# Fewer picked columns at the end of a layer, and their bank emptied earlier, in a three-layer graph attention kernel

## The reference

```python
h = relu(layernorm(x))
for l in range(3):
    f_out = (nf @ W_ni)[src] + (nf @ W_nj)[dst] + ef @ W_fij + bias
    f_out = leaky_relu(f_out, 0.2).reshape(-1, 4, 32)
    e = einsum('ehd,hd->eh', f_out, attn)
    a = exp(e - segment_max(e, dst)[dst]);  a = a / segment_sum(a, dst)[dst]
    m = (nf @ W_node).reshape(-1, 4, 32)[src] * a[:, :, None]
    nf, ef = segment_sum(m, dst).mean(axis=1), f_out.mean(axis=1)
out = x + nf
```

## Time and profile before

| | |
|---|---|
| median of 3 runs | 3021.41 us (3011.55 to 3023.02) |
| the profiled execution's own time | 3008.55 us |
| its span, first to last instruction | 3006.7 us |
| instructions | 50077 |
| TensorE's mean granted clock | 0.843 of 2.4 GHz |
| gathers (L554) | 1995, 1889.3 us busy |
| pick matmuls (L664) | 6345, 630.0 us busy |
| make_hot compares (L1360) | 705, 181.1 us busy |
| pick_rows copies (L1374, L1378) | 141 and 564, 33.0 and 155.3 us busy |

### The profile page before, as it was taken

One profiled execution on the slowest core, in us unless ns is written; L12 is line 12 of the kernel. 1 busy time (PEld: TensorE's weight loads), 2 busy tenths in 40 slices (PEclk: granted clock), 3 DMA queues, 4 the chain that ended last, 5 costly groups with the idle time before them and its releaser, 6 DMA issues.

```text
span 3006.7 us, 50077 instructions
## 1 busy us (share of the span) xinstructions
PE 2404.8 (80%) x15871; PEld 1878.0 (62%) x16027; DVE 2490.5 (83%) x6428; ACT 1447.6 (48%) x3416; POOL 2058.9 (68%) x2167
## 2 busy tenths in 40 slices
PE   3388888888887378888888887649999888998984
PEld 1366667676764356667766665337777777776753
DVE  7399999999997468998999998637888888879784
ACT  0155555555555135555556555414445454445452
POOL 6777777777770577777777776377776666667653
PEclk9699988888899589987999999857778787778796
DMA  6235454535342324343435342332333343333222
GB/s 252 64 96 156 122 147 116 152 110 158 110 128 85 112 74 142 119 149 110 157 111 158 110 153 98 118 103 67 100 120 99 98 136 98 108 108 100 91 92 81
DMA packets 139275, 353.92 MB, mean 118 GB/s; under 512 B 43895, under 2 KB 96027, under 8 KB 120207
## 3 DMA queue, kind: packets, MB, share of 16 engines
q1 hardware_dynamic: 67216, 296.09, 27.9%
q0 software_dynamic: 68960, 39.71, 8.6%
q10 hardware_dynamic: 2838, 14.91, 1.3%
HBM read 137.79 MB, written 212.77 MB: 117 GB/s over the span
## 4 chain that ended last, share of the span: by engine, by line
PE 39%; DVE 29%; issue 14%; ACT 9%; POOL 5%; DMA 3%; SPq 1%; DVEq 0%; ACTq 0%; POOLq 0%
DVE U L1349 12%; PE f_ps L695 12%; PE pick_ps L664 10%; PE f_ps L704 9%; PE xT_ps L685 5%; DVE rows L1266 4%; DVE lr L1277 4%; DVE U L1334 3%; POOL rows L554 2%; ACT f_low L850 2%; ACT xT L841 2%; ACT up L901 2%; PE f_ps L714 2%; ACT wide_ps L889 1%; DVE rows L1378 1%
## 5 line engine op out<-in xcount | busy, mean ns | idle before, releaser
L554 POOL DMA_INDIRECT rows<-nf_tab,src_sb x1995 | 1889.3, 947 | 706.9 <-issue 574.9
L704 PEld LDWEIGHTS f_ps<-w_out,lr 128*128 128x128 f32 x4836 | 701.0, 210 | 379.0 <-issue 277.3
L664 PE MATMUL pick_ps<-nf_part,z 125*128 125x160 bf16 x6345 | 630.0, 264 | 258.4 <-issue 217.0
L1349 DVE TENSOR_TENSOR_SCAN U<-wide_ps,U 128x272 f32<-128x272 f32 (+2 forms) x1272 | 801.6, 694 | 3.2 <-ACT wide_ps L889 2.4
L695 PE MATMUL f_ps<-xT,w_edge 97*128 97x512 f32 x1212 | 753.8, 708 | 22.6 <-ACT ef_new L872 12.0
L664 PEld LDWEIGHTS pick_ps<-nf_part,z 125*128 125x128 bf16 x6345 | 564.6, 112 | 289.8 <-issue 241.3
L704 PE MATMUL f_ps<-w_out,lr 128*128 128x36 f32 (+1 forms) x4836 | 649.8, 274 | 31.2 <-DVE lr L1277 28.8
L1277 DVE TENSOR_TENSOR lr<-f_ps,f_low 128x512 f32<-128x512 f32 x606 | 410.0, 677 | 252.4 <-ACT f_low L850 247.0
L850 ACT ACTIVATE f_low<-f_ps 128x512 f32<-128x512 f32 x606 | 361.0, 596 | 495.9 <-PE f_ps L695 495.9
L685 PE MATMUL xT_ps<-ident,rows 128*97 128x128 f32 x2418 | 431.8, 305 | 76.8 <-issue 37.2
L841 ACT ACTIVATE xT<-xT_ps 97x512 f32<-97x512 f32 x606 | 358.8, 592 | 147.8 <-PE xT_ps L685 145.6
(11 more groups left out here) (163 smaller groups left out, 1070.5 us busy)
## 6 DMA issues: line engine op xcount, KB each, us to landing
u_tab<-up SPq DMA_DIRECT2D x144, 1088.0 KB
s_nd<-edge_first SPq DMA_DIRECT2D x48, 768.0 KB
rows<-nf_tab,src_sb POOLq DMA_INDIRECT x1995, 2.5
ef_tab<-ef_new SPq DMA_DIRECT2D x32, 768.0 KB
ef_st<-ef_tab SPq DMA_DIRECT2D x32, 768.0 KB
z<-fifth_tab SPq DMA_DIRECT2D x141, 96.0 KB
edge_first<-s_nd ACTq DMA_DIRECT2D x16, 768.0 KB
ef_st<-in_edge_attr_dram SPq DMA_DIRECT2D x16, 672.0 KB
```

The source lines that it names most:

```text
L554: eng.indirect_dma_start(rows[q % RING][:, c * K:c * K + D], None, nf_tab[:, :], bass.IndirectOffsetOnAxis(ap=src_sb[:, t:t + 1], axis=0)) ...
L664: mm = eng.matmul(pick_ps[:, i * PB:(i + 1) * PB], hot[m % 2][0:NQ, f * PW + i * P:f * PW + (i + 1) * P], nf_part[a][0:NQ, f * PB:(f + 1) ...
L704: mm = eng.matmul(f_ps[n % 2][:, u * m:(u + 1) * m], lr[y][:, u * P:(u + 1) * P], w_out[l][:, 0:m], start=True, stop=True)
L1349: last = eng.tensor_tensor_scan(uh[:, c0 * w:c1 * w], dbc[h % 2][:, 0:(c1 - c0) * w], uh[:, c0 * w:c1 * w], 0.0, ALU.mult, ALU.add)
```

## The change

`PICK_LESS = [12, 2, 2]`: in layer 0 the last 12 of the 47 sub-blocks with picks have none, in layers 1 and 2 the last two. So `NPICKS` is 35, 45 and 45. GpSimd gathers those columns (48 more in all), and TensorE runs `warm` in those steps. The running number of a picked sub-block, on which buffers and semaphore values rest, comes from `pick_no`. On VectorE `pick_rows` is put right behind `leaky` of step i = 2, ahead of the two `add_up`; it was behind them.

```diff
@@ -31,6 +31,7 @@
 PARTS5 = 5
 SPLITS = 3
 IDXB = 4
+PICK_LESS = [12, 2, 2]
 SLOPE = 0.2
 WARM_UP = 16
 KEEP_WARM = 4
@@ -66,6 +67,7 @@
     HALF = [(0, D // 2), (D // 2, C)]
     END = NG - 18
     NPICK = END // GB + 1
+    NPICKS = [NPICK - PICK_LESS[l] for l in range(L)]
     assert NCOL == PARTS5 * PARTS5
     assert NQ * NCOL == N and HD == P and FULL < P and E < P * T
 
@@ -336,17 +338,20 @@
         def ef_in_count(q):
             return 16 * sum(ef_loads(a) for a in range(q % 2, q + 1, 2))
 
-        def picks(g):
-            return g % GB < PICK and g // GB < NPICK
-
-        def is_picked(t):
-            return t % GT == 2 and picks(t // GT)
-
-        def gathered(g):
-            return grp_w(g) - picks(g)
+        def picks(l, g):
+            return g % GB < PICK and g // GB < NPICKS[l]
+
+        def pick_no(l, b):
+            return sum(NPICKS[:l]) + b
+
+        def is_picked(l, t):
+            return t % GT == 2 and picks(l, t // GT)
+
+        def gathered(l, g):
+            return grp_w(g) - picks(l, g)
 
         def rows_sem_to(q, a):
-            return 16 * sum(gathered((v % NS) * GS + a)
+            return 16 * sum(gathered(v // NS, (v % NS) * GS + a)
                             for v in range(q % RING, q + 1, RING)
                             if (v % NS) * GS + a < NG)
 
@@ -413,7 +418,7 @@
                                   ).then_inc(ef_out[q % 2], 16)
 
                 def load_fifths(l, b):
-                    m = l * NPICK + b
+                    m = pick_no(l, b)
                     if m >= IDXB:
                         eng.wait_ge(hot_made, PARTS5 * (m - IDXB + 1))
                     eng.dma_start(fifths[m % IDXB],
@@ -494,7 +499,7 @@
                             load_ef(q0 + s + 2)
                         for b in range(max(SUBS * s - 2, 0), SUBS * s + 1):
                             store_u(k0 + b)
-                            if b + IDXB + 2 < NPICK:
+                            if b + IDXB + 2 < NPICKS[l]:
                                 load_fifths(l, b + IDXB + 2)
                     for b in range(SUBS * (NS - 1) + 1, NB):
                         store_u(k0 + b)
@@ -540,7 +545,7 @@
                 def gather_cols(l, cols):
 
                     for t in cols:
-                        if is_picked(t):
+                        if is_picked(l, t):
                             continue
                         q, c = l * NS + t // SUP, t % SUP
                         if c == 0 and q >= RING:
@@ -675,8 +680,8 @@
                             eng.wait_ge(dst_spread, (q + 1) * D)
                             eng.wait_ge(ef_put, q + 1)
                         eng.wait_ge(src_rows[q % RING][a], rows_sem_to(q, a))
-                        if picks(g):
-                            eng.wait_ge(picked, PARTS5 * (l * NPICK + g // GB + 1))
+                        if picks(l, g):
+                            eng.wait_ge(picked, PARTS5 * (pick_no(l, g // GB) + 1))
                         if n >= 2:
                             eng.wait_ge(xT_ready, n - 1)
                         else:
@@ -720,7 +725,7 @@
                     for g in range(-2, END - 2):
                         turn(g + 2)
                         b, i = g // GB + 2, g % GB
-                        if g >= 0 and i < PICK and b < NPICK:
+                        if g >= 0 and i < PICK and b < NPICKS[l]:
                             pick(b, i)
                         elif g >= 1:
                             warm(g + 1, FILL_STEADY)
@@ -1390,6 +1395,8 @@
                     for g in range(-1, END - 2):
                         b, i = g // GB - 1, g % GB
                         leaky(g + 1)
+                        if g >= 0 and i == PICK - 1 and b + 3 < NPICKS[l]:
+                            pick_rows(b + 3)
                         if b >= 0:
                             if i == 0:
                                 soften(b)
@@ -1401,9 +1408,7 @@
                             else:
                                 add_up(b, 2)
                                 add_up(b, 3)
-                        if g >= 0 and i == PICK - 1 and b + 3 < NPICK:
-                            pick_rows(b + 3)
-                        if g >= 0 and i == 0 and b + 4 < NPICK:
+                        if g >= 0 and i == 0 and b + 4 < NPICKS[l]:
                             make_hot(b + 4)
                         if 0 <= g and g // GS + 1 < NS:
                             s, a = g // GS + 1, g % GS
```

## The result

The changed kernel takes 3062.09 us (median of 4 runs, 3060.42 to 3065.61) against 3016.48 us before (median of 4, 3006.20 to 3023.02): ratio 1.0156, interval 1.0121 to 1.0191. It is slower, as forecast, by 46 us and not by 91. The time lies in the range of 3030 to 3180.

A forecast was written before the change was run, and what follows sets the result against it. VectorE was taken to bound the steady part at full clock. Move 82 + TensorE's gap 20 - removed picks 11 = +91 us on 3008.55, 3100; with the median's 12.9 above it, 3112 us, range 3030 to 3180.

The forecast's parts named there:

- What bounds the kernel: Steady part: VectorE is the bound at full clock, busy 47.0 of 48.9 us a triple (three sub-blocks); its waits are paid.
- The move at full clock: VectorE before leaky: 0.72 us lost a sub-block with spread_dst, 1.37 without, 2.8 a triple; upper bound 109 us.
- The move in layers 0 and 1: VectorE's delay by the moved pick_rows in these layers: 2.5 us a triple, 62 us.
- The move in layer 2: VectorE's delay there, half absorbed in its waits for slow TensorE: 1.4 us a triple, 20 us; at least 0.
- TensorE's gap: TensorE's stand moves behind pick, 2.45 us in place of 1.75; slow clock costs +20 us, at most 116.
- The 16 sub-blocks without picks: Last sub-blocks (12, 2, 2): VectorE's freed work gains 2.1 us a triple, -11 us; bounds 0 and -43.
- GpSimd's 48 gathers: GpSimd, 36 added in layer 0: cost nothing, with 84 us in hand there and 26 in layer 1.
- Rival 1: TensorE's stand for the emptied bank vanishes, clock stays 2.4 GHz: 128 us back, 139 with picks, 2882 us; chance 0.09.

The follow-up runs named there:

- e5: Kernel before plus one VectorE multiplication with unused result (some 0.8 us) behind each pick_rows, in all layers, pick_rows not moved: 3022.37 us, ratio 1.0055.
- e2: Kernel before with only the picks of the last 12, 2 and 2 sub-blocks removed, pick_rows still behind the add_ups: 3011.02 us, ratio 1.0017.
- e3: Kernel before with pick_rows moved, all picks kept, and ScalarE's two widens of step i = 3 put behind take_scores: 2906.67 us, ratio 0.9671.
- e1: Kernel before with only pick_rows moved ahead of the two add_ups, all picks kept: 3076.68 us, ratio 1.0237.
- e10: Kernel before plus the unused VectorE multiplication (0.8 us) behind pick_rows in layer 2 alone, nothing moved: 2982.69 us, ratio 0.9896.
- e9: Kernel before with pick_rows moved in layer 2 alone, all picks kept: 2980.52 us, ratio 0.9892.
- e6: Changed kernel with TensorE's filler matmuls of the picks-free steps in the empty pick bank: 3048.81 us, ratio 1.0157 to the kernel before.
- e8: Kernel before with picks removed, pick_rows moved, step i = 3's widens behind take_scores, picks-free filler in the empty pick bank: 2880.12 us, ratio 0.9593.
- e4: Kernel before with only ScalarE's two widens of step i = 3 put behind take_scores, pick_rows not moved: 3037.99 us, ratio 1.0119.

## Why the prediction was off by half

- **What bounds the kernel**: right at full clock. There more work of VectorE is paid (the shortest triple of layer 1 takes 51.1 us in e5, with 2.3 us more work, for 48.8 before), but averaged over a layer only about half of it or less is paid in layers 0 and 1, and none in layer 2 (e5). Where VectorE has less to do ahead of a wait for ScalarE, nothing is gained (e2).
- **The move at full clock**, 0.72 and 1.37 us a sub-block through ScalarE's widen: right. The waits are 0.65 and 1.48 us in the rows above, and e3 makes the loss vanish by ScalarE's order alone.
- **The move in layers 0 and 1**, 2.5 a triple and 20 us of clock on top, 3.3 together: 2.6 and 2.7 (e1 against the earlier trace rows; 1.8 and 2.3 in layer 1 if e10 and e9 are the measure). So 0.6 too much was forecast; 24.7 triples make that 16 us, or more by that scatter.
- **The move in layer 2, the step that failed.** "Half in layer 2, 1.4 a triple or 20 us", with nothing as the least it could cost. It measured -1.6 a triple, 14 x 1.6 = 22 us gained: 42 us off, most of the miss. I let VectorE's waits absorb a delay, at best all of it. The runs showed that the waits themselves shrink: in e10, 29 us of plain work took 63 us of waiting away, with TensorE's stand in place, and in e9 the move, in this layer alone, took 26 us off its triples and 26 off that wait.
- **TensorE's gap** moves behind pick and grows: right, 2.36 us in the row above. That longer gaps cost clock, the +20, isn't shown in any layer: in layers 0 and 1 the clock was 0.87 and 0.88, but e10, with the shorter gap there, has 0.88 and 0.87; in layer 2 it rose by 0.07 with the longer gap. The length of the stand alone doesn't set the clock.
- **The 16 sub-blocks without picks**, -11 us, of which 8.4 in the last four triples of layer 0. The gain there was 1.7 us (203.1 for 204.8), and nothing in e2. I had them at 46.8 us a triple, and they take 50.8. ScalarE's chain behind soften was but a part of the reason. The rest is the slow clock, as TensorE's filler waits for ScalarE: e6 takes that wait away and these triples come down by 12 us, to 47.8. I had costed the filler's wait at nothing, within the clock term.
- **GpSimd's 48 gathers**: nothing to be seen; e8, which has them too, is the fastest version.
- **Rival 1** has the clock coming back, which happened in part in layer 2, but not by its mechanism: the stand didn't go. With ScalarE's order changed too (e3), the clock comes back in all three layers; that gives 95 us in the profile (2911.6 for 3006.7), three quarters of the 128 that I had worked out for it.

The two mis-sized terms of the move make 58 us, and the picks' gain that didn't come gives 7 back: 91 - 58 + 7 = 40, for 39.6 measured in the 40 triples. The agreement is closer than layer 1's scatter of 12 us allows, so some of it is luck. The 17.5 us outside, which the sum didn't have, make it +57 in the profiles.

What stays open: why a later VectorE gets TensorE a better clock. e5 and e10 show that it does so in layer 2; that TensorE then has no arrears to make up behind a slow stretch is my reading of it, and no run isolates it. e4's loss is open as well.

## What to carry to other kernels

Before an instruction is moved on one engine, look what stands on the *other* engine behind the wait for what it was moved past: here a widen queued ahead of lower turned a 1.37 us swap into a stall, and putting the widen last turned the same swap from 2.4% slower into 3.3% faster. Where a layer waits for an engine whose clock is throttled, idle time there needn't be a fixed sum that a delay can at best hide in: time it, layer by layer, since one edit can gain in one layer and lose in the next. Freed work pays only when the next wait is taken away too (the same work removed gave nothing in layer 0 of e2 and 13 us in that of e8). And before a few us in one layer are read from a profile, look at that layer in a kernel that leaves it alone: here it moved by 12 us.

## What the runs showed of the hardware that was not expected

An addition of 45 useless VectorE instructions of 0.89 us to layer 2 made the whole kernel 1.0% faster (0.9896, 0.9853 to 0.9940), with TensorE's granted clock in that layer at 0.87 for 0.79, though TensorE did the same work and stood as often for the bank. And in the changed kernel TensorE's clock was still at 2.4 GHz for the edges right behind a stand of 2.36 us (1.10 us); the turn that started 1.95 us after it took 1.15 us, for the 0.66 of a turn at 2.4 GHz.
